# A gated attention and feed-forward kernel: gated values taken first, x turned behind the keys' mix, and one more batch transposed by TensorE

## What is computed

```
# layer 1: cross attention, 16 heads of 32 features, causal and masked
x = x + tanh(g_xattn) * attention(layernorm(x), ctx, ctx, mask, Wq, bq, Wk, bk, Wv, bv, Wo, bo)
# layer 2, on h = layernorm(x), with h_prev the token before (zero for the first)
hr = mu_r * h + (1 - mu_r) * h_prev
hk = mu_k * h + (1 - mu_k) * h_prev
r  = sigmoid(hr @ W_r.T)
k  = square(relu(hk @ W_k.T))
x  = x + tanh(g_ffn) * r * (k @ W_v.T)
```

## Time and profile before

| | before |
|---|---|
| median of 3 runs | 1903.14 us (1901.87 to 1903.62) |
| the profiled execution | 1903.74 us |
| its span, first to last instruction | 1902.0 us |
| mean granted TensorE clock | 0.993 |
| PE busy | 1851.3 us (97%) |
| PE weight loads busy | 1450.1 us (76%) |
| DVE busy | 1362.9 us (72%) |
| ACT busy | 1069.5 us (56%) |
| POOL busy | 1136.6 us (60%) |

### The profile page before, as it was taken

The page is one execution under the profiler, slowest core; times in us unless marked ns, Lnnn a source line. Parts: engine busy times, 40 slices in busy tenths (PEclk is TensorE's granted clock), DMA queues, the critical chain, the costliest instruction groups (busy, mean ns, idle before and its releaser), DMA issues.

```text
span 1902.0 us, 35167 instructions
## 1 busy us (share of the span) xinstructions
PE 1851.3 (97%) x10912; PEld 1450.1 (76%) x10912; DVE 1362.9 (72%) x3736; ACT 1069.5 (56%) x2051; POOL 1136.6 (60%) x1833
## 2 busy tenths in 40 slices
PE   6999999999999999999999999998989999999999
PEld 5677777777777777777777777776768788787887
DVE  6776767776776776767767776777576877868764
ACT  5655555555555655556555555556655646556452
POOL 2776777777777776777777777776533224232231
PEclk9999999999999999999999999998989999999999
DMA  7455465445545455464554655463445353453521
GB/s 219 104 131 130 126 160 124 121 126 136 154 113 138 121 140 133 111 167 116 121 133 128 155 122 128 121 165 95 133 118 149 99 146 112 111 156 99 145 67 67
DMA packets 162154, 244.38 MB, mean 128 GB/s; under 512 B 23056, under 2 KB 53776, under 8 KB 161200
## 3 DMA queue, kind: packets, MB, share of 16 engines
q1 hardware_dynamic: 161968, 242.12, 49.4%
HBM read 92.06 MB, written 33.59 MB: 66 GB/s over the span
## 4 chain that ended last, share of the span: by engine, by line
PE 85%; DVE 8%; issue 3%; ACT 2%; DMA 1%; SPq 1%; ACTq 0%; DVEq 0%
PE proj_ps L41 15%; PE proj_ps L42 15%; PE proj_ps L43 15%; PE score_ps L1435 10%; PE prob_ps L1459 8%; PE value_ps L1478 8%; DVE tiles L1148 3%; PE sum_ps L1486 2%; DVE x_io L1044 2%; DVE mix_k_low L1154 1%; PE score_ps L41 1%; PE score_ps L43 1%; PE score_ps L42 1%; PE value_ps L41 1%; ACT tiles L745 1%
## 5 line engine op out<-in xcount | busy, mean ns | idle before, releaser
L1078 DVE CUSTOM_DVE_ANT_0 score_ps<-score_ps,causal 128x128 f32<-128x128 f32 (+3 forms) x1024 | 488.8, 505 | 292.5 <-PE score_ps L1435 292.3
L687 ACT ACTIVATE probs<-prob_ps 128x512 f32<-128x512 f32 (+1 forms) x768 | 396.7, 529 | 370.4 <-PE sum_ps L1486 184.0
L1435 PE MATMUL score_ps<-k_stack,q_stack 97*128 97x128 f32 (+3 forms) x1024 | 318.2, 352 | 4.5 <-DVE least L1078 3.3
L1459 PE MATMUL prob_ps<-q_stack,k_stack 100*128 100x512 f32 (+3 forms) x1024 | 279.9, 314 | 3.1 <-DMA q_stack<-max_rows 3.0
L492 POOL TENSOR_TENSOR prob_sum<-probs 128x384 f32<-128x384 f32 x256 | 259.9, 1015 | 0.0
L1435 PEld LDWEIGHTS score_ps<-k_stack,q_stack 97*128 97x128 f32 x1024 | 187.2, 189 | 74.8 <-issue 40.8
L495 POOL TENSOR_TENSOR prob_sum<-prob_sum,probs 128x256 f32<-128x256 f32 x256 | 198.2, 774 | 37.0 <-POOL prob_sum L492 0.4
L1459 PEld LDWEIGHTS prob_ps<-q_stack,k_stack 100*128 100x128 f32 x1024 | 191.7, 190 | 22.5 <-DMA q_stack<-max_rows 3.6
L481 POOL TENSOR_SCALAR_AFFINE_SELECT probs<-probs 128x256 f32<-128x256 f32 x256 | 105.0, 410 | 152.0 <-ACT probs L687 151.7
L530 POOL TENSOR_SCALAR newton<-moments 128x4 f32<-128x4 f32 x14 | 8.7, 621 | 290.4 <-DVE moments L1052 290.4
L485 POOL TENSOR_SCALAR_AFFINE_SELECT probs<-probs 128x256 f32<-128x256 f32 x256 | 106.7, 417 | 126.0 <-ACT probs L687 126.0
(11 more groups left out here) (180 smaller groups left out, 4811.7 us busy)
## 6 DMA issues: line engine op xcount, KB each, us to landing
k_stack<-staged SPq DMA_DIRECT2D x384, 128.0 KB
q_stack<-staged SPq DMA_DIRECT2D x384, 128.0 KB, 3.1
x_io<-in_x SPq DMA_DIRECT2D x16, 1024.0 KB, 7.8
x<-x_io SPq DMA_DIRECT2D x64, 256.0 KB, 3.1
res<-x SPq DMA_DIRECT2D x64, 256.0 KB, 3.6
out_x<-res SPq DMA_DIRECT2D x64, 256.0 KB, 5.3
tiles<-in_x SPq DMA_DIRECT2D x15, 1024.0 KB, 5.5
tiles<-in_ctxT SPq DMA_DIRECT2D x60, 256.0 KB, 4.1
```

The source lines that it names most:

```text
L687: nc.scalar.activation(probs[:, u % RING, lo:hi], prob_ps[(3 * u + c) % 2][:, 0:hi - lo], ACT.Exp, scale=SCALE).then_inc(exp_done, 1)
L1078: nc.vector.tensor_tensor_reduce(out=here, in0=here, in1=causal[:, LATE - P * t:S], scale=-1.0, scalar=3e38, op0=ALU.add, op1=ALU.min, acc ...
L1435: last = nc.tensor.matmul(here[:, at:at + P * (t + 1)], q_stack[n][0:MASK_ROW + 1, j, P * t:P * t + P], k_stack[n][0:MASK_ROW + 1, j, 0:P ...
L1459: last = nc.tensor.matmul(here[:, at:at + width], k_stack[n][0:ROWS, j, P * k:P * k + P], q_stack[n][0:ROWS, j, P * k:S], start=True, stop ...
```

## The change

Five things, all in the second layer:

1. Batch 2 joins batches 0 and 1: its x comes by one load and is transposed by TensorE among batch 1's key products (two token tiles behind group 2, two behind group 3), with four copies on ScalarE. Turning and moving by DMA begin with batch 3 (BY_DMA).
2. VectorE turns x behind the keys' mix, no longer in its middle.
3. VectorE takes each tile's gated values as the first thing of each step of the receptance mix, and adds them a step later.
4. ScalarE normalises x behind the keys' mix and behind the tanh of tile 2.
5. GpSimd makes the first two low parts of the squared keys ahead of the inversion, for every batch from 1 on.

The diff, without the constants and some waits' counts that follow from item 1:

```diff
-        ffn_xT = {j: x_room[0] if j < 2 else attn_room[j % 2] for j in range(B)}
+        ffn_xT = {j: x_room[0] if j < BY_DMA else attn_room[j % 2] for j in range(B)}
...
                 elif b == B + 2:
                     sp.wait_ge(xt_done, T * b)
-                elif b == B + 3:
+                elif b == B + BY_DMA:
                     sp.wait_ge(o_done, T * B)
+                elif b == B + BY_DMA + 1:
+                    sp.wait_ge(xt_done, T * (b - 1))
                 elif b > B:
-                    sp.wait_ge(x_turned, T * (b - B - 3))
+                    sp.wait_ge(x_turned, T * (b - B - BY_DMA - 1))
...
-                if b > B + 1:
+                if b >= B + BY_DMA:
                     for a in range(QUARTERS):
...
                 if j == 1:
-                    move_x(2)
                     load_x(B + 4)
                 if j + 2 < B:
                     move_x(j + 2)
...
             for j in range(1, B):
+                low_part_act(j, 0)
+                low_part_act(j, 1)
                 if j + 2 < B:
                     invert_deviations(B + j + 2)
-                for g in range(K):
-                    low_part_act(j, g)
+                low_part_act(j, 2)
+                low_part_act(j, 3)
...
                 high_part_act(j, 0)
                 relu_k(j, 2)
+                if j == 1:
+                    copy_x(2, 0)
+                    copy_x(2, 1)
                 high_part_act(j, 1)
                 relu_k(j, 3)
+                if j == 1:
+                    copy_x(2, 2)
+                    copy_x(2, 3)
                 high_part_act(j, 2)
...
                 if j + 1 < B:
                     high_part_mix(e + 1)
-                if j + 2 < B:
-                    for m in range(T):
-                        apply_layernorm(B + j + 2, m)
                 if j + 1 < B:
                     scale_earlier(e + 3)
                     high_part_mix(e + 2)
                 gate_r(j, 2)
                 if j + 1 < B:
                     high_part_mix(e + 3)
+                if j + 2 < B:
+                    for m in range(T):
+                        apply_layernorm(B + j + 2, m)
                 gate_r(j, 3)
...
                 low_part_mix(e + 1)
+                mix_tokens(e + 3)
+                low_part_mix(e + 2)
+                low_part_mix(e + 3)
                 if turn_too:
                     for m in range(T):
                         turn_x(j + 1, m)
-                mix_tokens(e + 3)
-                low_part_mix(e + 2)
-                low_part_mix(e + 3)
-
-            def mix_r_and_combine(j, done):
+
+            def mix_r_and_combine(j):
 
                 e = 2 * K * (j + 1) + K
+                gate_values(j, 0)
                 mix_tokens(e)
-                for k in range(1, K):
+                mix_tokens(e + 1)
+                low_part_mix(e)
+                for k in range(2, K):
+                    gate_values(j, k - 1)
+                    add_values(j, k - 2)
                     mix_tokens(e + k)
                     low_part_mix(e + k - 1)
-                    if k - 1 >= done:
-                        combine(j, k - 1)
+                gate_values(j, K - 1)
+                add_values(j, K - 2)
                 low_part_mix(e + K - 1)
-                combine(j, K - 1)
+                add_values(j, K - 1)
...
-                if j == 1:
-                    square_k(j, 1)
-                    for m in range(T):
-                        turn_x(2, m)
-                elif j + 2 < B:
+                if j > 1 and j + 2 < B:
                     take_stats(B + j + 2)
-                if j > 1:
-                    square_k(j, 1)
+                square_k(j, 1)
                 square_k(j, 2)
...
                     for k in range(K):
                         project_fk(j, g, k)
+                    if j == 1 and g in (2, 3):
+                        transpose_x(B + 2, 2 * (g - 2))
+                        transpose_x(B + 2, 2 * (g - 2) + 1)
```

More of the change, by code:

```diff
@@ L71, in gated_layer @@
     SIDE, QUARTERS = 32, 4
+    BY_DMA = 3
+    MOVES = 16 * QUARTERS * QUARTERS
     assert T == 4 and K == 4 and HG == 4 and H == 16
@@ L316, in move_x @@
             def move_x(j):
-                sp.wait_ge(x_turned, T * (j - 1))
-                if j < 4:
+                sp.wait_ge(x_turned, T * (j - BY_DMA + 1))
+                if j < BY_DMA + 2:
                     sp.wait_ge(o_done, T * B)
@@ L736, in scale_earlier @@
                 j, n, k = mix_tile(e)
-                if j < 2:
+                if j < BY_DMA:
                     act.wait_ge(xt_copied, T * (j + 1))
                 else:
-                    act.wait_ge(x_moved, 16 * QUARTERS * QUARTERS * (j - 1))
+                    act.wait_ge(x_moved, MOVES * (j - BY_DMA + 1))
                 act.wait_ge(zeroed, 1)
@@ L1038, in turn_x @@
                 dve.wait_ge(ln_applied, T * (B + j) + m + 1)
-                if j == 2:
+                if j == BY_DMA:
                     for n in range(T):
@@ L1412, in _ @@
                     mix_k(j + 1, j + 2 < B)
-                    mix_r_and_combine(j, 0)
+                    mix_r_and_combine(j)
                 else:
@@ L1552, in transpose_x @@
                 elif b > B:
-                    pe.wait_ge(xt_copied, T + m - 1)
+                    pe.wait_ge(xt_copied, T * (b - B) + m - 1)
                 elif m != 1:
```

6 lines of the change are left out of this document (3 added, 3 removed).

## The result

The changed kernel takes 1877.74 us (median of 4 runs, 1877.37 to 1878.92) against 1903.08 us (4 runs, 1901.87 to 1903.62): a ratio of 0.9869, 95% interval 0.9852 to 0.9886. The forecast was 1876.9 us, with a range of 1874 to 1885. The profiled execution took 1877.37 us, its span is 1875.6 us, its mean granted clock 0.996.

A forecast was written before the change was run, and what follows sets the result against it. The prediction took TensorE, busy 1851.3 of 1902.0 us, and its waits as the bound. Gains of 15.9 + 10.3 + 0.6 = 26.8 us off the profiled 1903.74 gave 1876.9 us, range 1874 to 1885.

The forecast's parts named there:

- term A: Batches 2 to 13: with gated values first on VectorE, TensorE's waits for them go, 12 x 1.33 = 15.9 us.
- Rival (b): Batches 2 to 13: gates stay late behind VectorE's turning of x, each keeping its 1.33 us; 1892.8 us, chance 0.05.
- Rival (c): Batches 2 to 13: value products wait for GpSimd's last low parts behind a slow inversion; slower, 1920.0 us, chance 0.03.
- term B: Batch 1: transposing batch 2's x on TensorE regains 14.1 us and costs 3.8, net 10.3 us.
- Rival (a): Batch 1 regains less: its two transpose pauses take the clock down and the load is slower; 1884.4 us, chance 0.11.
- term C: Ahead of batch 1's key products: one load for four of batch 2's x lets VectorE run earlier, 0.6 us.

The follow-up runs named there:

- dve_busier1: The changed kernel with one extra VectorE operation (about 0.7 us) between the turning of x and the first gate: 1877.93 us (0.9863).
- norms_3us: The changed kernel with five extra ScalarE copies (some 3.0 us together) ahead of the layer norms of batch 2's x: 1880.53 us (0.9876).
- four_loads: The changed kernel with batch 2's x read by four loads of 256 KB in place of one of 1024 KB: 1878.39 us (0.9864).
- dve_busier: The changed kernel with four extra VectorE operations (some 0.7 us each) between the turning of x and the gate of tile 0: 1903.06 us (1.0002).
- gates_late: The changed kernel with item 3 undone, so VectorE makes two mixes and a low part ahead of the gate: 1900.87 us (0.9991).
- batch2_only: The kernel before with item 1 alone, batch 2's x by one load and sixteen transposes, other orders as before: 1894.59 us (0.9959).

## Why the prediction was right, and where it was not

**The gates (term A).** Forecast 12 x 1.33, measured 12 x 1.32. The cause is settled from both sides: item 3 alone brings 15.8 us, and without it they are gone. The way to it was less exact. I had the gate of tile 0 end at 1620.2 in before's clock, 1.8 us ahead of its due time; it ended at 1603.62, that is 1621.1, with 0.9 to spare, and 1.6 us behind its products' end instead of 0.7. The step that was off is the mix's end. I had the remaining two mixes and three low parts end "at about 1616.5", but my own terms give 1609.86 + 2.49 + 1.78 + 5 x 0.7 = 1617.6, an error of adding; they ended at 1600.20, or 1617.7. VectorE's last mix was therefore late too, behind a mix of 1.58 and a low part of 1.78 us beside GpSimd, and ScalarE's last high part stood 1.47 us for it (1598.85). I had it end at 1615.8, before that mix was due by the right sum; it ended at 1616.9, and norms (forecast to end 1618.8, ended 1619.8), turning (1619.5 and 1620.5) and gate are each one microsecond late behind it. So I put too much trust in items 2 and 4: with them undone the gate comes 0.69 us sooner, and the time is the same. `dve_busier1` shows how thin the cover is.

**Rival (b) and the rule on the ports.** Rival (b) did not come, but with 0.9 us of spare time it was closer than I said. GpSimd's two low parts run from 1593.86 to 1597.39 here; beside them VectorE ended a low part and a mix and did most of another low part, the last two some 0.8 and 1.1 us longer than alone, and GpSimd's own took 3.53 us in place of 2 x 1.29. By the Trainium skill (SBUF — State Buffer, section "SBUF: two separate sides"), VectorE and GpSimd hold the shared ports exclusively for a whole instruction. VectorE was not shut out until the last low part's end, as I had read the rule, and the gate came 0.9 us ahead of the 1622.0 worked out by it. That the two took turns, instruction by instruction, would fit these rows about as well as a mere slowing; no run here tells them apart.

**GpSimd's low parts.** I rated item 5 at 0. For batches 2 to 13 that holds. In batch 1 it is worth 2.1 us, which I missed because I costed it in batch 7 and not in the batch where the inversion is slow. Even so, one wait stays: the third low part ends at 1401.71 + 1.70 = 1403.4 and the last at 1405.12, and the product at 1405.17 started 0.52 us behind the one before it, in place of 0.23. Rival (c) named this very wait, for batches 2 to 13; it came in batch 1 alone and at 0.3 us, since the inversion took 7.0 us there (1394.70 to 1401.7) and 5.6 in batch 7 (1588.25 to 1593.86). In batch 7 the last low part ended at 1597.39, that is 1614.9, where 1614.4 was forecast and 1618.6 would do.

**Batch 1 (term B).** Forecast 14.1 - 3.8 = 10.3, measured 9.86. The receptance products start 3.67 us later behind the first key product than before (14.92 us against 11.25), where I had 3.8. That sum is right by two errors: the waits are 0.84 + 0.48 = 1.32 and not 2.0, but the sixteen transposes with their restarts cost 2.5 and not 1.8 (the two places together 3.82, of which 0.09 fall behind the first receptance product), and 0.06 came back at short waits ahead of them. The 96 products behind them take 22.31 us and not 21.76; of the 0.55, some 0.4 are the wait for GpSimd's last low part and the restart behind it. Rival (a) held the clock to be in danger at pauses near 1.9 us. The first was 2.1 us, the second 1.5 (gaps of 1.23 + 1.09 and 0.87 + 0.90 us, less the 0.23 of a product), and the clock stayed at 1.00. The danger was real, though: in each of the two kernels with a wait of 1.5 to 1.9 us in every batch from 2 to 13, one batch lost the clock for eight products. The price that I gave it, 2.3 us, is 1.6 there and 1.3 in `norms_3us`.

**The load (term C).** Forecast 0.6, measured 0.50, and the reason was wrong. `four_loads` starts its key products as early. So it was not the number of loads; what is left is their form, which I did not try by itself: before, each load filled 32 partitions with four rows apiece (`"(m c) d -> c m d"`), 6.5 us to the last; four loads of 128 rows on 128 partitions take 6.0, one takes 5.9. Over all kernels the mark is followed by batch 1's first key product after 27.41 to 27.56 us with the old loads (three kernels) and after 26.91 to 27.34 with the new, so 0.4 is the better figure. The form of the load as the cause is what the other runs leave, and is not shown.

**The sum.** 26.2 us from the three terms, where 26.8 was forecast; 0.58 from layer 1 that no term explains, and -0.34 in the last batches and the end. The total was as good as it was (0.8 us off) partly by luck: layer 1's share happened to fill the gap of 0.6, and I took the gain off the profiled 1903.74 us, which is 0.7 above the median of 1903.08. By the medians the gain is 25.3 us, 1.5 less than forecast.

## What to carry to other kernels

Read a short wait that recurs as a question of order: which instruction stands ahead of the one waited for, and could it stand behind? Here another order of a dozen lines on VectorE gave 15.8 us without taking away any work, and the reorderings around them (turning and norms later) gave none. Cost each item in every stage that differs from the rest: item 5 was free of effect in twelve batches and worth 2.1 us in the thirteenth. And test the spare time by loading the engine with a known step; a forecast with the right total may rest on a spare time that is half of what you think.

## What the runs showed of the hardware

- A wait of the same length may or may not take TensorE's clock down. Of twelve waits of 1.75 us in `dve_busier`, one was followed by a granted clock of 0.5, the lower of the two levels (1.2 GHz), for some 3.4 us; of twelve in `gates_late`, eleven of 1.53 were not and one of 1.90 was. In both, the first five or six products behind the wait still ran at the upper level. The twenty-four waits of 1.00 in before and `batch2_only` and single ones of 1.46 to 1.50 in four kernels were never followed by it; one of 3.17 was at once.
- A wait costs more than its length: 1.00 us cost 1.32 of pitch, 1.53 cost 1.86, 1.75 cost 2.06. It is 0.32 us each time, for the restart.
- The inversion, sixteen small operations on GpSimd, took 5.6 us in the changed kernel's batch 7, 7.0 in its batch 1 and 9.8 ahead of before's; single steps of 0.20 us became 0.5 to 0.7 while VectorE was busy. In before's batch 1, where VectorE was busy for 0.5 of 4.8 us, fifteen of the sixteen steps took 0.2 us and the whole 4.8.
- Layer 1, the same code in all, ended between 1348.1 and 1350.8 us in the profiled executions. Differences of 1 to 2 us between kernels have to be read behind a mark in the trace and not from the medians.
